# Gate logits formed in the prepare stage, means by TensorE matmuls, and a new order of the prepare stage and of the mixture's biases

## The reference: what is computed

```python
x = x + L0_xattn(layernorm(x), ctx);  x = x + L0_attn(layernorm(x));  x = x + L0_ffn(layernorm(x))
... # L1 the same; L2_attn is convolution, pooled keys, a dense "boom"; L3_ffn holds a grouped attention and a mixture
# mixtures of experts (L0_ffn: 8 experts, top 2; L1_ffn: 16, top 3; L3_ffn: 8, top 2; L2_ffn picks by a sequence's first token)
logits = x @ gate (+ gate_b);  out = sum over the chosen experts of weight * (act(x @ w1 + b1) @ w2 + b2)
# L2_attn, between its convolution and its boom, with h = layernorm(x) * g + b
q, k, v = h @ Wq.T + bq, h @ Wk.T + bk, h @ Wv.T + bv
scale = arange(1, S + 1)
pooled_q = cumsum(q, axis=1) / scale
pooled_k = cumsum(pooled_q * k, axis=1) / scale
x = x + pooled_k * v
```

## Time and profile before

| | us |
|---|---|
| median of 3 runs | 2048.44 (2044.97 to 2049.84) |
| the profiled execution, its own time | 2051.6 |
| its span, first to last instruction | 2049.7 |
| PE busy | 1629.8 (80%) |
| DVE busy | 988.8 (48%) |
| ACT busy | 749.4 (37%) |
| POOL busy | 448.5 (22%) |
| mean granted TensorE clock | 0.844 of 2.4 GHz |

### The profile page before, as it was taken

The page is one execution under the profiler, slowest core; times in us unless marked ns, Lnnn a source line. Parts: engine busy times, 40 slices in busy tenths (PEclk is TensorE's granted clock), DMA queues, the critical chain, the costliest instruction groups (busy, mean ns, idle before and its releaser), DMA issues. The chain is left out here.

```text
span 2049.7 us, 53611 instructions
## 1 busy us (share of the span) xinstructions
PE 1629.8 (80%) x22017; PEld 1400.3 (68%) x22017; DVE 988.8 (48%) x2108; ACT 749.4 (37%) x1700; POOL 448.5 (22%) x627
## 2 busy tenths in 40 slices
PE   5999746769994999795799579987288978878684
PEld 4888645669993777574688569974277956666574
DVE  5655373331116888626321447763855744344413
ACT  3555262224441555332233236652223322333222
POOL 3443102012222443210344122210101200010241
PEclk9999865569996999766799879998697989776797
DMA  4111000059862211001699633320101154000486
GB/s 149 50 54 29 5 1 4 4 195 329 328 255 94 57 47 49 6 3 66 227 313 318 205 129 101 91 61 0 44 12 45 41 184 132 4 2 4 164 305 202
DMA packets 81733, 220.56 MB, mean 108 GB/s; under 512 B 19128, under 2 KB 35000, under 8 KB 74112
## 3 DMA queue, kind: packets, MB, share of 16 engines
q1 hardware_dynamic: 73376, 195.37, 29.0%
q0 software_dynamic: 8160, 22.29, 2.9%
HBM read 202.22 MB, written 15.34 MB: 106 GB/s over the span
## 5 line engine op out<-in xcount | busy, mean ns | idle before, releaser
L2273 PEld LDWEIGHTS ps<-xt,w 128*128 128x128 f32 x1728 | 207.7, 196 | 37.6 <-issue 30.9
L2273 PE MATMUL ps<-xt,w 128*128 128x128 f32 x1728 | 215.2, 281 | 20.4 <-DMA w<-in_L_ffn_w 17.7
L2323 ACT ACTIVATE g<-ps,b 128x128 f32<-128x128 f32 x340 | 125.0, 368 | 248.8 <-PE ps L2273 227.4
L2283 PE MATMUL ps<-w,g 128*128 128x256 f32 x864 | 201.1, 380 | 0.8 <-DMA w<-in_L_ffn_w 0.8
L2283 PEld LDWEIGHTS ps<-w,g 128*128 128x128 f32 x864 | 157.9, 191 | 19.1 <-ACT g L2323 1.0
L2356 POOL DMA_INDIRECT x<-rows,token x85 | 83.2, 979 | 262.9 <-DVEq L2455 237.9
L2361 POOL DMA_INDIRECT results<-y,dest x85 | 83.7, 985 | 258.4 <-DVE y L2488 258.4
L2480 DVE COPY xt<-ps 128x256 f32<-128x256 f32 x85 | 36.1, 425 | 206.2 <-PE ps L2263 206.2
L409 PE MATMUL ps<-x,w 128*128 128x512 f32 x408 | 110.4, 429 | 20.2 <-DVE x L572 20.2
L2488 DVE COPY y<-ps 128x256 f32<-128x256 f32 x85 | 36.1, 424 | 161.9 <-PE ps L2283 161.9
L409 PEld LDWEIGHTS ps<-x,w 128*128 128x128 f32 x408 | 82.7, 208 | 41.1 <-DVE x L572 24.3
(11 more groups left out here) (445 smaller groups left out, 3640.0 us busy)
## 6 DMA issues: line engine op xcount, KB each, us to landing
w<-in_L_ffn_w SPq DMA_DIRECT2D x124, 512.0 KB, 5.1
w<-in_L_ffn_w SPq DMA_DIRECT2D x46, 1024.0 KB, 5.2
c<-in_ctx SPq DMA_DIRECT2D x96, 258.0 KB, 2.9
rows<-in_w_L_xattn SPq DMA_DIRECT2D x32, 192.0 KB, 2.5
rows<-in_w_L_xattn SPq DMA_DIRECT2D x8, 768.0 KB
c<-in_w_L_xattn SPq DMA_DIRECT2D x8, 514.0 KB
back<-results SPq DMA_DIRECT2D x16, 256.0 KB, 5.2
raw<-in_L_ffn_w SPq DMA_DIRECT2D x16, 256.0 KB, 2.8
```

What stands on the lines that cost most here:

```text
L2273: mm = nc.tensor.matmul(hidden_bank(par, h), b.w1[:, par, c, h * P:(h + 1) * P], b.xt[:, par, c, :], start=c == 0, stop=c == DC - 1)
L2283: mm = nc.tensor.matmul(k.ps[:, YB + par, 0:D], b.g[:, par, h, :], b.w2[:, par, h, :], start=h == 0, stop=h == HC - 1)
L2323: nc.scalar.activation(b.g[:, par, h, :], hidden_bank(par, h), func, bias=b.b1[:, par, h:h + 1]).then_inc(s.g_ready, 1)
```

## The change

1. In `prepare` with `known`, TensorE turns both halves before the first product; ScalarE and VectorE split the second half before they take the first product. GpSimd waits until the 8 norms (4 in the first stage) are done before it splits weights or clears.
2. For L0_ffn, L1_ffn and L2_ffn the logits are formed at the end of `prepare`, with the gate as the stationary operand: 4 fp32 matmuls of 512 columns, a copy of each half by ScalarE, and 8 small transposes into PSUM bank 6. L3_ffn keeps the old form, in bank 6.
3. In the biased mixtures the shares are turned and spread before the first block; the 8 bias matmuls stay behind the last block and signal in two halves, and VectorE adds a half before each four tiles. In all three mixtures the summation goes by pairs of tiles.
4. At the end of `ffn` the statistics of the last but one group stand before the last adds.
5. The queries, keys and values of L2_attn are token-major with biases as rows. `pool_keys` averages with a 128x128 matrix on TensorE, adds to z and takes the statistics; its transpose stage goes. `keep` and `rcount` and their late load go; `mean` (64 KB) joins the first load.

```diff
 # prepare: TensorE
             turn(0)
+            if known:
+                turn(1)
             if units:
                 product(0, 0)
-            turn(1)
+            if not known:
+                turn(1)
...
+            if logits is not None:
+                E = logits.shape[2]
+                pe.wait_ge(*w_at)
+                for half in range(2):
+                    pe.wait_ge(s.ht_c0, half + 1)
+                    pe.wait_ge(s.ht_c1, half + 1)
+                    for c in range(DC):
+                        mm = nc.tensor.matmul(k.ps[0:E, 4 + half, :], logits[:, c, :], ht[:, c, half * 512:(half + 1) * 512],
+                                              start=c == 0, stop=c == DC - 1)
+                    mm.then_inc(s.logits_done, 1)
+                for t in range(NT):
+                    pe.wait_ge(s.logits_taken, t // HT + 1)
+                    nc.tensor.transpose(k.ps[:, 6, t * E:(t + 1) * E], l.logits[:, t * P:(t + 1) * P], k.ident[0:E, 0:E])
 # prepare: ScalarE
             deviation(1)
+            if known and units:
+                take_turned(1)
...
+                    nc.scalar.copy(l.logits[:, tokens], k.ps[0:logits.shape[2], 4 + half, :]).then_inc(s.logits_taken, 1)
 # prepare: GpSimd
+            pool.wait_ge(s.norm_done, NT if known else HT)
             for n, w in enumerate(ws):
 # prepare: VectorE
                 split(0)
...
+                if known:
+                    split(1)
                 take_product(0, 0)
-                split(1)
+                if not known:
+                    split(1)
 # ffn: VectorE
+                    if last and j == UNITS - 1:
+                        note(it, j - 1)
                     add(it, j)
                     if last and j == UNITS - 1:
-                        note(it, j - 1)
                         note(it, j)
 # mixture: TensorE
             pe.wait_ge(s.idx_ready, 1)
+            if b1 is not None:
+                pe.wait_ge(s.comb_ready, 1)
+                nc.tensor.transpose(k.ps[0:W, YB + 1, 0:P], f.comb[:].rearrange("p t e -> p (t e)"), k.ident).then_inc(s.comb_turned, 1)
             turn(0, 0, 0)
+            if b1 is not None:
+                pe.wait_ge(s.comb_spread, 1)
 # mixture: VectorE
+            def add_biases(half):
+                dve.wait_ge(s.bias_done, half + 1)
+                tiles = into[:, 4 * half:4 * half + 4, :].rearrange("p (h a) d -> p h (a d)", a=2)
+                nc.vector.tensor_tensor(tiles, tiles, k.ps[:, HB + 2 * half:HB + 2 * half + 2, :], ALU.add).then_inc(s.bias_added, 1)
...
+            for pair in range(0, NT, 2):
+                if b1 is not None and pair % 4 == 0:
+                    add_biases(pair // 4)
                 for n in range(top):
+                    for t in (pair, pair + 1):
+                        if n == 0:
+                            dve.wait_ge(returned[t], 16)
+                        else:
+                            dve.wait_ge(s.summed, pair * top + 2 * n - 1 + t - pair)
 # pool_keys
-def pool_keys(k, q, key, v):
+def pool_keys(k, q, key, v, into):
+            for pair in range(PAIRS):
+                for t in range(2):
+                    mm = nc.tensor.matmul(k.ps[:, pair, t * D:(t + 1) * D], k.mean, q[:, 2 * pair + t, :, 0:16], start=True, stop=True)
+                mm.then_inc(s.queries_averaged, 1)
+            for pair in range(PAIRS):
+                pe.wait_ge(s.keys_ready, pair + 1)
+                for t in range(2):
+                    mm = nc.tensor.matmul(k.ps[:, PAIRS + pair, t * D:(t + 1) * D], k.mean, b.keys[:, 2 * pair + t, :],
+                                          start=True, stop=True)
+                mm.then_inc(s.keys_averaged, 1)
...
+            for pair in range(PAIRS):
+                dve.wait_ge(s.queries_averaged, pair + 1)
+                weigh(b.keys, pair, key, pair).then_inc(s.keys_ready, 1)
+            for pair in range(PAIRS):
+                dve.wait_ge(s.keys_averaged, pair + 1)
+                weigh(b.values, PAIRS + pair, v, pair).then_inc(s.values_ready, 1)
+                if pair:
+                    add(pair - 1)
+                if pair > 1:
+                    note(pair - 2)
+            note(PAIRS - 2)
+            add(PAIRS - 1)
+            note(PAIRS - 1)
 # the calls
-                        prepare(k, k.x, k.z, ht=k.ht, known=True)
+                        prepare(k, k.x, k.z, ht=k.ht, known=True, w_at=w.at, logits=w.gate)
...
-                        pool_keys(k, f.q, f.key, f.v)
-                        transpose_channels(k, f.v, k.z, k.z)
+                        prepare(k, k.z, b.hn, token_major=[(f.q, w.wq, w.bq), (f.key, w.wk, w.bk), (f.v, w.wv, w.bv)],
+                                gain=w.g2, shift=w.b2, w_at=w.at, known=True)
+                        pool_keys(k, f.q, f.key, f.v, k.z)
```

More of the change, by code:

```diff
@@ L163, in packs @@
                       ("conv", conv_blocks(g("conv_w")))] + \
[L164 removed]
+                     [(a, row(g(a))) for a in ("bq", "bk", "bv")] + \
+                     [(a, column(g(b))) for a, b in (("cb", "conv_b"),
                                                      ("g1", "ln_conv_g"), ("b1", "ln_conv_b"), ("g2", "ln_attn_g"),
@@ L317, in load_early @@
     fetch_weights(k, sp)
-    if not k.late_started:
-        k.late_started = True
-        sp.dma_start(k.consts[:, k.late:], k.in_const[:, k.late:]).then_inc(k.late_loaded, 16)
     if early:
@@ L325, in prepare @@
 def prepare(k, src, z, ht=None, padded=None, jobs=(), token_major=(), gain=None, shift=None, w_at=None,
-            early=(), clear_early=None, fold=None, ahead=(), known=False, once=None):
+            early=(), clear_early=None, fold=None, ahead=(), known=False, once=None, logits=None):
     nc = k.nc
@@ L355, in prepare @@
         b = ctx.enter_context(buffers(k, std=[P, NT], rstd=[P, NT], std1=[P, NT], rstd1=[P, NT], std2=[P, NT]))
-        if jobs:
+        if ws:
             r = ctx.enter_context(buffers(k, F32R, x=[P, 2, DC, T], w=[P, 2, DC, starts[-1]]))
-        if jobs and gain is not None:
+        if logits is not None:
+            l = ctx.enter_context(buffers(k, logits=[logits.shape[2], T]))
+        if ws and gain is not None:
             f = ctx.enter_context(buffers(k, x=[P, DC, T]))
@@ L482, in take_turned @@
                         if gain is None:
-                            nc.scalar.copy(out, inp)
+                            nc.scalar.copy(out, inp).then_inc(s.ht_c0, 1)
                         else:
@@ L527, in _ @@
                 take_product(0, 0)
-            take_turned(1)
+            if not (known and units):
+                take_turned(1)
             for n in range(1, len(units)):
@@ L532, in _ @@
                 take_product(1, n)
+            if logits is not None:
+                for half in range(2):
+                    tokens = slice(half * 512, (half + 1) * 512)
+                    act.wait_ge(s.logits_done, half + 1)
+                    nc.scalar.copy(l.logits[:, tokens], k.ps[0:logits.shape[2], 4 + half, :]).then_inc(s.logits_taken, 1)
         @block.gpsimd
         def _(pool):
+            pool.wait_ge(s.norm_done, NT if known else HT)
             for n, w in enumerate(ws):
@@ L1807, in _ @@
         def _(pe):
-            pe.wait_ge(*w.at)
-            for t in range(NT):
-                for c in range(DC):
-                    mm = nc.tensor.matmul(k.ps[:, 0, t * E:(t + 1) * E], k.ht[:, c, t * P:(t + 1) * P], w.gate[:, c, :],
-                                          start=c == 0, stop=c == DC - 1)
-            mm.then_inc(s.logits_done, 1)
             if kind in ("sequence", "capacity"):
@@ new lines, in add, with note @@
+            def add(pair):
+                dve.wait_ge(s.values_ready, pair + 1)
+                tiles = into[:, 2 * pair:2 * pair + 2, :]
+                nc.vector.tensor_tensor(tiles, tiles, b.values[:, 2 * pair:2 * pair + 2, :], ALU.add).then_inc(s.added, 1)
+            def note(pair):
+                dve.wait_ge(s.added, pair + 1)
+                for t in range(2 * pair, 2 * pair + 2):
+                    nc.vector.bn_stats(k.stats[:, t, :], into[:, t, :]).then_inc(s.noted, 1)
+            for pair in range(PAIRS):
+                dve.wait_ge(s.queries_averaged, pair + 1)
+                weigh(b.keys, pair, key, pair).then_inc(s.keys_ready, 1)
@@ new lines, in _ @@
+            for pair in range(PAIRS):
[8 more added lines that the diff above has]
+            note(PAIRS - 1)
+            for t in range(NT):
+                dve.wait_ge(s.noted, t + 1)
+                nc.vector.bn_aggr(k.mv[:, t, :], k.stats[:, t, :])
@@ L2871, in build @@
                     early = [(raw.raw1[:], w1[0]), (raw.raw2[:], w2[0])]
-                    prepare(k, k.x, k.z, ht=k.ht, early=early, known=True)
+                    prepare(k, k.x, k.z, ht=k.ht, early=early, known=True, w_at=w.at, logits=w.gate)
                     with buffers(k, comb=[P, NT, n_exp], comb_t=[n_exp, T]) as b:
```

122 lines of the change are left out of this document (50 added, 72 removed).

## The result

The changed kernel takes 2000.19 us (median of 4 executions, 1991.09 to 2002.01), the one before 2047.49 us (4 executions, 2044.97 to 2049.84) on the same chip. The ratio is 0.976, 95% interval 0.9728 to 0.9793: 47.3 us less. Measured once more later, the same kernel took 1997.48 us (ratio 0.9749, 0.9728 to 0.9771).

The account below looks back on a forecast made before the run. The kernel was taken as a row of stages waiting for one another, no engine busy over four fifths; 16.2 + 2.5 + 11.1 + 4.7 + 1.8 + 0 - 0.35 - 0.2 = 35.8 us less gave 2012.6 us, range 2002 to 2026.

Parts of the forecast that it names:

- First product 4.5 us after the norms, norms in 2.67: Prepare stages with known statistics: norms last 2.67 us and the first product comes 4.5 us after their start.
- the forecast's 1.8 more: L2_attn's prepare: 1.8 us added for one more cast and a split with both inputs in SBUF.
- The slow first stretch: Projecting prepare stages: units start at low clock, 4.5 us at half speed, about 2.0 us lost (1.3 to 2.8).
- What a stage takes besides its units: Projecting prepare stages: 0.57 + 4.5 + 2.0 + 1.0 = 8.0 us on top of the units.
- First stage 2.5: The kernel's first prepare stage: norms no longer run beside GpSimd's subtracting and clearing, gain 2.5 us.
- pool_keys, 14.4 after: pool_keys with its transpose stage: 25.50 us before, 14.4 after, gain 11.1 us.
- Mixture ends 4.7: Ends of the mixtures: gain 2.5 us in L0_ffn, 1.7 in L1_ffn, 0.5 in L3_ffn.
- Logits, zero: Logits of L0_ffn, L1_ffn and L2_ffn: 0.8 us gained twice, 1.6 lost once, zero in sum (-4 to +4).
- Notes 1.8: Ends of both ffn stages: statistics and aggregates move under the wait for the last products, gain 1.8 us in sum.
- (c): Rival for the whole kernel: the clock rises early and nothing collides, 2000 us; chance 0.17.

Follow-up runs that it names:

- old turns: The changed kernel with the second half's turn, split and rounding moved back behind the first unit or take, GpSimd still waiting for the norms: 2016.55 us, ratio 0.9838.
- after: The kernel with the whole change, against the kernel before: 2000.19 us, ratio 0.976; measured again unchanged, 1997.48 us, ratio 0.9749.
- started warm: The kernel with biases first, plus four identity transposes at the head of each of the seven projecting stages: 1995.67 us, ratio 0.9751.
- biases first: The changed kernel with both bias halves added before the first pair of tiles: 1996.3 us, ratio 0.9752; again 1993.99 us, ratio 0.9736.

## Why the prediction was too high

By its own steps:

- **First product 4.5 us after the norms, norms in 2.67:** 4.51 in four of the seven stages, 4.28 in L3_gqa. In L2_xattn the product waited for GpSimd's longer remainder and came at 5.26, as forecast (0.7 too late); in L2_attn it came at 6.16, and the forecast's 1.8 more was right too.
- **The slow first stretch:** this is the step that failed. "I take 4.5 us at half speed, 3 to 6 as ends: about 2.0 lost (1.3 to 2.8)" was about 0.3 in L1_attn (5.92 against 5.63) and 0.1 in L1_xattn (four units in 5.75). TensorE's clock was up within some 0.5 us of the first product's start, not 4.5 us behind it. What a stage takes besides its units was put at 8.0; L0_attn, L1_xattn, L1_attn, L3_attn and L3_gqa had 6.2, 6.3, 6.2, 6.1 and 6.0. Over these five that is 9.3 us of the 11.0 missing in the seven; L2_attn gave 1.8 more in one profile and 0.2 in the other. L2_xattn alone was as forecast (20.0 against 19.9): there the clock rose late and the first two units took 2.70 and 2.07, some 2.0 too much, but in five other measurements of the new order they ran at the high clock and the stage took 18.0. The 2.0 came from PEclk and the first unit of the old stages, as if the low clock belonged to the start of a stage. It went with what TensorE had done there: 8 transposes, then 2.07 us of standing still (4.13 in L2_attn, 2.46 in L2_xattn). The change fills that stretch with 8 more transposes, and filling it with useless ones gives back much of the same (7.4 of the 21.4 us between old turns and after, 7.3 in the kernel before). Of the other 14 (11.5 against the second measurement of after), L2_attn holds 5.7: 2.0 are the earlier first product (8.16 against 6.16), the rest is a turn that no longer stands between products and first units at the high clock. In the six others it is 0.7 to 2.2, 1.4 on average; a turn of 8 transposes, which the new order no longer puts between products, is 1.03 in L1_attn.
- **The two rules it leaned on.** The Trainium skill, page "TensorE: Matmul & The Clock Gate", section "What's actually happening", says that the low state is the default and activity releases it; the trace agrees: the same unit took 1.82 behind transposes that filled the gap and 2.93 behind the gap. The Trainium skill, page "SBUF — State Buffer", section "Who interferes with whom", was used for the split, which kept its 1.29 us beside GpSimd in after, as in the earlier trace rows. Its other half, that `tensor_scalar` can take the port pair which GpSimd needs and that one of the two then blocks fully, fits the norms: 5.51 against 2.67.
- **First stage 2.5:** 2.0 and 2.8 measured (19.1 and 18.3 against 21.1); right.
- **pool_keys, 14.4 after:** 13.35. The first loop ended at 4.4 as said. In the second, adds and weighings follow each other 0.60 apart, not 0.7, and TensorE had the high clock: gain 12.15 against 11.1.
- **Mixture ends 4.7:** L0_ffn 2.9 (2.5 forecast), L1_ffn 1.8 (1.7); in L3_ffn, whose mixture wanders from 146.9 to 155.7 us over all kernels, nothing can be read.
- **Logits, zero:** under-sized, the second step that failed. They were worth 4.5 to 7.2 us by medians and up to 8.2 by stages. L0_ffn's logits were put at half high clock, 4.9, and ran at 3.60: here too the forecast kept TensorE at the low clock for too long. And L1_ffn was counted as a loss of 1.6 from the one row of 4.16 us; the old form took 6.98 there in three other kernels, and the new one 4.45, a gain of 2.5.
- **Notes 1.8:** right in sign, 0.7 to 2.4 measured.

Added up, the seven stages give 24.8 to 27.2, the first 2.0, pool_keys 12.15, the ends 4.7, the notes 0.7 to 2.4 and the logits 4.5 to 8.2: 49 to 57, where the two measurements of after gave 47.3 and 50.4. The untouched stages of after's first profile are 4.2 us longer than before's, those of its second 2.5 shorter. Stage by stage the two first profiles do close: 27.2 in the seven, 2.0 in the first, 12.15 in pool_keys, 7.2 in L0_ffn, 1.0 in L1_ffn, 3.9 in L2_ffn and 3.0 in L2_boom's ffn, less 4.2 in the untouched stages, 1.4 in L2_boom's prepare, which waits for its loads, and 1.1 in L3_ffn: the 50.0 between the spans. What sets the clock in those stages from one kernel to the next stays open: L3_attn's self attention, untouched, had PEclk 0.73 before and 0.64 after, and took 56 to 58 us in the three kernels built on before and 59.7 to 62.6 in ten of the eleven built on after (56.8 in the one started warm), which no run here explains.

Of the rivals, (c), the clock rises early and nothing collides, at 2000, is what happened, with L2_xattn as the exception. It had 0.17; the earlier trace rows showed that units take 1.4 us once the clock is up, and the new order puts twice the work ahead of the first product.

## What to carry to other kernels

A stretch of little work and 2 us of idling ahead of the first product cost more than itself here, because the products behind it ran at half clock (2.93 us for a unit of 1.4); move work that has to be done anyway into the gap before pricing anything else. The early clock it gives is likely, not certain: L2_attn had it in one measurement of after and not in the next. Take the price of a short group of matmuls from more than one profile. When a low clock is read from a profile, ask what the engine was doing just before and whether the change alters that, instead of carrying the loss over as a fixed toll of the stage. Keep GpSimd off while VectorE's norms run (2.67 us alone, 5.51 beside it), and off a split with all operands in SBUF; and put an operation whose operands are early under a wait for a transfer, not behind it.

## What the runs showed of the hardware that was not expected

- A unit of six products took 2.93 us behind a gap of 2.07 us and 1.82 or 1.66 behind transposes that filled it, with no earlier start. Eight transposes per stage that nothing reads made the kernel before 6.8 us faster. Transposes alone can bring the clock up: in that kernel L1_attn's first unit, at 1.66, had a granted clock of 1.00 from its start, and only transposes had run in the stage before it. A gap of 2.01 us behind 16 transposes was followed by the high clock once and by the low clock once.
- VectorE's norms lost 2.84 us to 3.17 us of GpSimd work, the buffer clear included, while a subtraction with one input in PSUM lost nothing.
- A stage with the same instructions has preferred lengths: L2_xattn's prepare took 18.0 us in both measurements of biases first and 20.0 and 19.9 in those of after, with PEclk 0.88 and 0.75 in the first of each. Over all measurements of the new order it is 18.0 in five and 19.9 to 20.3 in five.
